# Windowed attention on one core: order of two row operations on VectorE and of the exponentials on ScalarE

## What is computed

```
win = xh.reshape(B, H // WS, WS, W // WS, WS, C).transpose(0, 1, 3, 2, 4, 5).reshape(-1, L, C)
qkv = (win @ qkv_w.T + qkv_b).reshape(-1, L, 3, HEADS, HD).transpose(2, 0, 3, 1, 4)
attn = jnp.einsum('bhld,bhmd->bhlm', q, k) * SCALE
attn = jax.nn.softmax(attn + bias[None], axis=-1)
out = jnp.einsum('bhlm,bhmd->bhld', attn, v).transpose(0, 2, 1, 3).reshape(-1, L, C)
out = out @ proj_w.T + proj_b
x_lpe = (conv2d(x, lpe_w, groups=C, pad=1) + lpe_b.reshape(1, C, 1, 1)) * lpe_scale * noise_mask
x_attn_img = x_attn.transpose(0, 3, 1, 2) + x_lpe
```

## Time and profile before

| what | value |
|---|---|
| median of 3 runs | 9218.36 us (9204.33 to 9221.74) |
| the profiled execution | 9222.4 us |
| its span, first to last instruction | 9220.8 us |
| mean granted TensorE clock | 0.931 |
| TensorE matmuls busy | 8240.3 us, 89% |
| VectorE busy | 5469.2 us, 59% |
| ScalarE busy | 5129.6 us, 56% |
| GpSimd busy | 4772.7 us, 52% |

### The profile page before, as it was taken

One profiled execution on the slowest core, in us unless ns is written; L12 is line 12 of the kernel. 1 busy time (PEld: TensorE's weight loads), 2 busy tenths in 40 slices (PEclk: granted clock), 3 DMA queues, 4 the chain that ended last, 5 costly groups with the idle time before them and its releaser, 6 DMA issues. The chain is left out here.

```text
span 9220.8 us, 265192 instructions
## 1 busy us (share of the span) xinstructions
PE 8240.3 (89%) x88874; PEld 6129.4 (66%) x88874; DVE 5469.2 (59%) x20355; ACT 5129.6 (56%) x16576; POOL 4772.7 (52%) x7513
## 2 busy tenths in 40 slices
PE   9998998999998999999898999899999989899930
PEld 8996666766676666666685667666666668566720
DVE  4554776467745775377646774477537774577410
ACT  5555664366644664366546664466436654666434
POOL 1112775177724774277616772477427762677300
PEclk9998998999989998999999998999899999999875
DMA  7551000200012000200020000200020002000089
GB/s 126 97 99 34 21 14 21 83 14 15 14 36 67 15 20 15 83 15 20 21 78 14 21 14 30 68 20 20 15 83 15 20 21 72 19 21 14 13 318 409
DMA packets 386950, 487.51 MB, mean 53 GB/s; under 512 B 249616, under 2 KB 352528, under 8 KB 369296
## 3 DMA queue, kind: packets, MB, share of 16 engines
q1 hardware_dynamic: 369488, 393.67, 14.9%
q0 software_dynamic: 16192, 77.49, 2.1%
HBM read 319.45 MB, written 151.66 MB: 51 GB/s over the span
## 5 line engine op out<-in xcount | busy, mean ns | idle before, releaser
L437 POOL TENSOR_SCALAR work<-work 128x128 f32<-128x128 f32 x5120 | 3575.3, 715 | 0.0
L950 PE MATMUL ps<-work 128*32 128x144 f32 (+4 forms) x32902 | 1823.7, 302 | 304.4 <-ACT work L545 89.3
L556 ACT ACTIVATE work<-work 128x144 f32<-128x144 f32 x5120 | 2043.4, 403 | 0.9
L802 DVE SCALAR_TENSOR_TENSOR work<-xs,lw,work 128x570 f32<-128x570 f32 (+1 forms) x2048 | 1655.1, 819 | 0.0
L950 PEld LDWEIGHTS ps<-work 128*32 128x32 f32 (+3 forms) x32902 | 1012.3, 127 | 905.9 <-issue 564.6
L766 DVE CUSTOM_DVE_ANT_0 work<-ps,negbias 128x144 f32<-128x144 f32 x5120 | 1247.2, 303 | 615.0 <-issue 431.0
L950 PE MATMUL ps<-work,wqkv 128*128 128x288 f32 x4096 | 1317.0, 446 | 109.1 <-POOL work L449 78.1
L433 POOL TENSOR_TENSOR work<-work 128x80 f32<-128x80 f32 x1024 | 437.5, 427 | 1345.9 <-DVE work L773 1338.6
L468 POOL TENSOR_TENSOR work<-work 96x384 f32<-96x384 f32 x512 | 421.0, 822 | 1109.8 <-DVE work L874 1109.8
L950 PEld LDWEIGHTS ps<-work,wqkv 128*128 128x128 f32 x4096 | 733.3, 197 | 393.8 <-POOL work L425 82.5
L556 ACT ACTIVATION_READ_ACCUMULATOR work<-work 128x1 f32 x5120 | 970.8, 190 | 0.0
(11 more groups left out here) (126 smaller groups left out, 12080.5 us busy)
## 6 DMA issues: line engine op xcount, KB each, us to landing
work<-in_x SPq DMA_DIRECT2D x128, 576.0 KB, 5.5
xs<-in_x SPq DMA_DIRECT2D x64, 1152.0 KB, 5.3
AH<-in_x SPq DMA_DIRECT2D x192, 384.0 KB, 3.4
y_scratch<-AH SPq DMA_DIRECT2D x192, 384.0 KB, 2.5
AH<-y_scratch SPq DMA_DIRECT2D x64, 1152.0 KB, 23.4
out<-AH POOLq DMA_DIRECT2D x64, 1152.0 KB, 17.7
xs<-in_x SPq DMA_DIRECT2D x112, 96.0 KB, 5.0
bias_scratch<-in_rpb_rev POOLq DMA_DIRECT2D x144, 4.5 KB, 2.1
```

What stands on the lines that cost most here:

```text
L437: o = g.tensor_scalar(sp[t % 4][:, c, L - 128:L], sp[t % 4][:, c, L - 128:L], rden[t % 4][:, c:c + 1], None, ALU.mult)
L556: o = act.activation(sp[t % 4][:, c, :], sp[t % 4][:, c, :], ACT.Exp, scale=-1.0, bias=mn[t % 4][:, c:c + 1], accum_out=den[t % 4][:, c:c ...
L802: v.scalar_tensor_tensor(dst[:, ct, :, w0:w1], xs[side][:, ct, y0 + dy:y0 + dy + HS, w0 + dx - 1:w1 + dx - 1], lw[:, ct, tap:tap + 1], dst ...
L950: return nc.tensor.matmul(o, l, r, start=start, stop=stop)
```

## The change

On ScalarE `exps(t + 2)` goes ahead of `o_out(t - 2)`. On VectorE the first two taps of a step are issued together, ahead of `row_masked`, and `row_added` follows `row_masked` directly; before, one tap stood ahead of the pair and one between. A third and later tap stay where they were, behind `recip`. Nothing else differs; every instruction that computes is still there, and no semaphore changes. Lines behind 843 stand three lower in the changed file, so TensorE's 950, 1085, 1088 and 1133 are there 947, 1082, 1085 and 1130.

```diff
@@ -583,10 +583,10 @@
                     for t in range(NT):
+                        if not (last and t + 2 >= NT):
+                            exps(t + 2)
                         if not (head and t < 2):
                             o_out(t - 2)
-                        if not (last and t + 2 >= NT):
-                            exps(t + 2)
                         made = pieces_at(t, last)
                         for i in made[:1]:
                             piece_out(i)
@@ -840,13 +840,10 @@
                         r = None if head else row_at(t)
-                        for half, k in steps[:1]:
+                        for half, k in steps[:2]:
                             lpe_step(half, k)
                         if r is not None:
                             row_masked(n - 1, r, psRow)
-                        for half, k in steps[1:2]:
-                            lpe_step(half, k)
-                        if r is not None:
                             row_added(n - 1, r, psRow, s * WS - WS + r)
                         if not (last and t + 2 >= NT):
                             recip(t + 2)
```

## The result

The changed kernel takes 8983.23 us (median of 4 runs, 8967.61 to 9038.09) against 9214.20 for the kernel before on the same chips: a ratio of 0.9765, 95% interval 0.9731 to 0.9799. The forecast was 8954 (ratio 0.971), in a range of 8890 to 9085. So the kernel is faster by 2.3%, and the forecast took off some 30 us too much.

What follows compares the result with a forecast made beforehand. TensorE was taken to bound the kernel. Terms of 185 + 55 + 12 + 12 = 264 us off the profiled 9222.4 gave 8958; with the median 4 us lower, the forecast was 8954 us, range 8890 to 9085.

Steps and rivals of the forecast that it cites:

- The bound and the two waits: TensorE sets the pace; its weight loads wait 162.4 us for line 818 (`row_added`) and 181.2 us for line 545 (evacuation).
- The cost of a wait: Behind step 7, TensorE loses 1.23 - 0.45 = 0.78 us each time, more than the 0.49 listed.
- VectorE's term: At 304 waits of TensorE for `row_added`, each gives back 0.61 of its 0.78 us: 185 us.
- `row_added` comes 1.13 - 0.52 = 0.61 us earlier: On VectorE, the pair takes 1.13 us start to start with a tap between and 0.52 without, if `row_masked` is unmoved.
- is `row_masked` unmoved?: In step 7 the second tap (0.80 us) just fits VectorE's 0.78 us idle time; the longest tap makes the pair 0.15 late.
- ScalarE's term: In steps 1 and 9 line 545 comes 0.43 us earlier, 55 us; other waits for 545 give 12 us.
- What is late next: TensorE's next transposes keep 0.27 us of margin to VectorE's copies (781); new waits for 437, 781 or 572 would refute it.
- Half the gain: Late taps or late normalised weights lose half of the 0.61 us: 9047 us, or 9102 without ScalarE's 55; chance 0.20.
- Slower: Taps held until GpSimd's running scalings end make `row_masked` up to 1.10 us late: 9312 us; chance 0.06.
- The whole wait goes: The residual 0.18 us wait for the bank closes too, 52 us more: 8902 us; chance 0.10.
- no change: What TensorE wins it waits for at the next semaphore, so no change is seen; chance 0.04.
- Signs: Expected in the changed profile: strip 79.5 us, 818 starting 0.52 behind 812, VectorE idle some 250 us ahead of 812.

Runs made afterwards that it cites:

- the fastest kernel: Changed kernel with the strips' loop written out on every engine and, in steps 5 and 13, the second tap behind the pair; 8848.15 us, ratio 0.9596.

## Why the prediction was right, and where its sizes were off

**The bound and the two waits: right.** TensorE set the pace. Each wait fell with its own edit and stayed with the other's.

**The cost of a wait, 0.78 us and not 0.49: right.** With the bank's delay gone altogether, steps 3 and 7 went from 5.21 to 4.43 us, by 0.78.

**VectorE's term: 185 us forecast, with 12 more in the last strips; 140 measured alone, 150 on top of ScalarE's edit.** The step that failed is "`row_added` comes 1.13 - 0.52 = 0.61 us earlier". The 0.52 was read in the earlier trace rows, from rows whose address is a constant; in the loop the pair stands 0.62 apart. That leaves 0.51, and steps 3 and 7 gained 0.48. In the last strips, where the row is a constant too, the same steps gained 0.60 (5.21 to 4.61), so the reading was right for its own form. The rows showed the difference: those of the earlier trace rows end in "96x256 f32<-96x256 f32", that of the earlier trace rows in "f32 x1". The second part was "is `row_masked` unmoved?" It is in steps 3 and 7; in step 5 it starts 0.09 late, within the 0.15 that I allowed but did not put into the sum. Of the 47 us between 197 and 150, the address accounts for some 27 (0.10 in 272 places) and the late pair for some 9, by estimate from the step times; the rest I cannot place.

**ScalarE's term: 67 us forecast, 55 + 12; 63 in the attention of that edit alone.** Steps 1 and 9 gained 0.40 to 0.41 of the 0.43 forecast. The head strips, which the forecast had given some 7 us and most of the 12, each got 2.6 us shorter, 21 us in all.

**The sum:** 264 us forecast, 213 in the attention, so 51 too many. Between the medians it is 231. Those 18 us more are not the forecast's merit but luck: they come from outside the attention or from the spread of the runs, since in the one profile of each kernel the rest of the program grew by 28 us. I had taken all that the change does not touch as constant, which it is not by some tens of us.

**What is late next: right.** None of the three came up: ahead of the transposes TensorE's matmuls waited 69.8 us for 781, after 66.2 before, and 21.4 us for 437, after 36.1; for 572 it stayed 5.5. In step 7 781 ended at 1136.10 and the next transposes began at 1136.38. With the tap behind the pair that margin was gone, and the wait for 781 rose to 147.7 us.

**The rivals.** *Half the gain* did not come, but both of its mechanisms were there in small: a late tap of 0.09, and GpSimd's scalings that lengthen two taps by 0.27. *Slower* needed a delay beyond 0.61. The rule of the Trainium skill ("SBUF — State Buffer", who interferes with whom) named the right pair of engines, and leaving the scalings out shows VectorE's side of it; but the price was 0.27 us for two taps together, not the 1.2 of two whole scalings. Nor did the one that starts second always wait for the whole of the first. In the kernel before, this tap starts 0.08 us behind the middle one of these three scalings (the second line, ns min/median/max), takes no longer than the median of its line, and the scaling is the one that grows, to 1.35 us:

```profile
1124.62 0.80 DVE L802 SCALAR_TENSOR_TENSOR work<-xs,lw,work 128x570 f32<-128x570 f32 x1
L437 POOL TENSOR_SCALAR work<-work x3: 597/598/1353, 1124.0 to 1125.9; 128x128 f32<-128x128 f32 x3
```

*The whole wait goes* falls, since 0.3 us a step stayed, and *no change* falls by the 2.3%.

**Signs.** The strip took 79.9 us for 79.5 forecast; VectorE's idle time ahead of 812 194 us for 250; step 9 lost 0.40 for 0.4; step 7 0.48 for 0.6. The pair stands 0.62 apart for 0.52, and j = 3 loads 0.32 behind the others for 0.2. The sign against me, that 812 no longer waits and starts late, came true for steps 5 and 13 by 0.09; in all, 812 waits in 264 places for 693.

## What to carry to other kernels

Price a moved pair of instructions by rows of the same form: here a destination that comes from a register added a sequencer's instruction, and as that one waited for the first operation, its time fell behind the wait. Where an engine waits with work in its queue that nobody needs soon, put that work into the wait, and issue what frees the other engine directly behind it; but see how long the work is against the wait, step by step, since the same tap was right ahead of the pair in steps 3 and 7 and better behind it in step 5. And read a bounding engine's loss from the distance between its instructions, not from the listed idle time.

## What the runs showed of the hardware

**A delay without idle time.** In step 7 of the changed kernel the two loads of j = 3 start 0.32 us behind the first of the other six. Those six fill most of that time, so the list counts no idle time for a loss of 0.31 us. The list of waits had fallen to 14.8 us while the run without `row_masked` shows 112 us of attention still to be had.

**The stage behind the attention has several lengths.** From an image's last 818 to the next image's first 766 the same instructions take mostly 282, 292 or 300 us. Three such stages (columns as above; 1890 weight loads in each), first two of the changed kernel, then one of the fastest:

```profile
3495.00:3795.00 300.00, 284.44 (x1890) 226.94 (x1890) 118.18 (x274) 112.82 (x222) 54.97 (x74) 0.88 0.24 74
5461.00:5753.00 292.00, 275.93 (x1887) 220.16 (x1890) 118.45 (x275) 112.30 (x222) 54.98 (x74) 0.90 0.24 76
```

```profile
3431.00:3713.00 282.00, 264.77 (x1887) 212.08 (x1890) 118.36 (x274) 112.25 (x222) 55.12 (x74) 0.95 0.25 79
```

The length goes with the mean granted clock, 0.88, 0.90 and 0.95, and the work is the same. The difference lies at the start of the stage. In 44 us just behind the attention (3497 to 3541, 5464 to 5508 and 3439 to 3483) the mean granted clock is 0.51, 0.73 and 0.96, and in the rest of the stage 0.94, 0.93 and 0.94. In the ten profiles the clock stays at the lower of its two levels there for 41 to 44 us in every stage of 298 to 300 us, for 20 to 27 us in those of 288 to 292, and for 3 to 7 us in those of 281 and 282. In the changed kernel's profile five of the seven stages are of the 300 kind; in the fastest kernel's one is, three are of 292 and three of 282. That is 58 us between two profiles that the attention does not account for (2082 against 2024), of the size of the spread within one kernel's runs (8967.61 to 9038.09). The fastest and the slowest of those had mean granted clocks of 0.934 and 0.925. What decides how long the clock stays low was not tried and stays open. In the kernel with the tap behind, all seven stages are of the longest kind and its five runs lie within 27 us, so it may depend on the kernel and need not be chance from run to run; that is not shown. A few tenths of a per cent in the ratios above can be of this origin, in either direction.
